# A depthwise sum held in one PSUM bank, strip by strip, and class sums that share one bank

## The reference: what is computed

```python
x = x + _L0_conv_ref(_gn(x), W_v, W_a, b_a, W_o, b_o)   # outlook attention
x = x + _L1_conv_ref(_gn(x), w)                         # depthwise 3 x 3, weights binarized
# inside _L0: v = x @ W_v; a = softmax(pool2x2(x) @ W_a + b_a) over 9 of 9 x 9 x 12 logits
#             out = a @ patches(v), folded back by overlap-add into y; y @ W_o + b_o
# inside _L1: k = sign(clip(w, -1, 1)); out = conv(x, k, 3 x 3, 'SAME', one filter a channel)
# _gn: (v - mean) / sqrt(var + eps) over groups of 3 channels of one image
```

## Time and profile before

| | |
|---|---|
| median of 3 runs | 5118.91 us |
| the profiled execution, its span | 5120.9 us |
| VectorE busy | 4730.3 us, 92% |
| TensorE busy | 4119.3 us, 80% |
| GpSimd busy | 4037.2 us, 79% |
| ScalarE busy | 2005.6 us, 39% |
| TensorE's granted clock, mean | about 0.85 of full speed |

### The profile page before, as it was taken

The page is one execution under the profiler, slowest core; times in us unless marked ns, Lnnn a source line. Parts: engine busy times, 40 slices in busy tenths (PEclk is TensorE's granted clock), DMA queues, the critical chain, the costliest instruction groups (busy, mean ns, idle before and its releaser), DMA issues.

```text
span 5120.9 us, 55367 instructions
## 1 busy us (share of the span) xinstructions
PE 4119.3 (80%) x13632; PEld 2114.1 (41%) x13632; DVE 4730.3 (92%) x3723; ACT 2005.6 (39%) x2753; POOL 4037.2 (79%) x3628
## 2 busy tenths in 40 slices
PE   4877887878887888878788887888878888878885
PEld 2434444434444344444344443444434444434442
DVE  5799999999999999999999999999999999999997
ACT  4424444334443344432444433444324444334431
POOL 5787877877877888778878788787787787887883
PEclk7988888888888788888888888888888888888887
DMA  1110111101111111111011111111110111111111
GB/s 39 38 38 24 47 44 37 47 21 40 47 33 47 36 25 47 42 39 47 21 40 47 33 47 30 31 47 38 43 47 15 46 47 33 47 24 37 47 29 28
DMA packets 126083, 194.36 MB, mean 38 GB/s; under 512 B 14248, under 2 KB 115464, under 8 KB 122472
## 3 DMA queue, kind: packets, MB, share of 16 engines
q1 hardware_dynamic: 97384, 155.50, 13.0%
q10 hardware_dynamic: 28672, 38.55, 2.5%
HBM read 39.22 MB, written 38.54 MB: 15 GB/s over the span
## 4 chain that ended last, share of the span: by engine, by line
POOL 45%; issue 25%; PE 18%; ACT 5%; DVE 5%; DMA 1%; SPq 0%; DVEq 0%; POOLq 0%; ACTq 0%; PEldq 0%; PEld 0%
POOL prod L363 15%; POOL part L356 10%; POOL att L351 10%; PE acc L753 10%; POOL att L345 6%; PE bc L733 4%; DVE prod L600 2%; ACT X L440 2%; POOL pc L332 2%; PE side L698 2%; ACT X L523 2%; PE side L692 1%; DVE ACC L647 1%; PE side L710 1%; DVE top L631 1%
## 5 line engine op out<-in xcount | busy, mean ns | idle before, releaser
L753 PE MATMUL acc<-prod,wo 96*96 96x392 f32 x5312 | 2478.5, 573 | 161.8 <-POOL prod L363 155.7
L600 DVE TENSOR_TENSOR prod<-bc,VAL 96x784 f32<-96x784 f32 x2048 | 1928.2, 959 | 307.5 <-PE bc L733 289.4
L363 POOL TENSOR_TENSOR prod<-prod 96x392 f32<-96x392 f32 x1440 | 1685.5, 1178 | 501.3 <-DVE prod L600 491.7
L733 PE MATMUL bc<-stack,sel 96*96 96x392 f16 x4608 | 1303.2, 378 | 633.5 <-DVE prod L600 611.5
L647 DVE SCALAR_TENSOR_TENSOR ACC<-XP,sg,ACC 96x1064 f32<-96x1064 f32 (+1 forms) x768 | 1736.2, 2281 | 14.9 <-ACT ACC L534 13.8
L753 PEld LDWEIGHTS acc<-prod,wo 96*96 96x96 f32 x5312 | 982.1, 188 | 675.1 <-issue 271.6
L733 PEld LDWEIGHTS bc<-stack,sel 96*96 96x96 f16 x4608 | 576.2, 137 | 1571.4 <-DVE prod L600 972.2
L351 POOL TENSOR_TENSOR att<-att,top 108x420 f32<-108x420 f32 (+1 forms) x576 | 750.3, 1321 | 38.3 <-ACT top L467 38.3
L345 POOL TENSOR_TENSOR att<-att,top 108x420 f32<-108x420 f32 (+1 forms) x576 | 645.1, 1138 | 144.2 <-DVE top L623 144.2
L356 POOL TENSOR_TENSOR part<-att,part 108x420 f16<-108x420 f32 (+1 forms) x576 | 737.3, 1298 | 0.0
L433 ACT ACTIVATE att<-side,ba 108x420 f32<-108x420 f32 (+1 forms) x576 | 340.5, 597 | 671.6 <-PE side L698 659.0
(11 more groups left out here) (55 smaller groups left out, 2183.7 us busy)
## 6 DMA issues: line engine op xcount, KB each, us to landing
stack<-part SPq DMA_DIRECT2D x192, 275.3 KB
stack<-part SPq DMA_DIRECT2D x192, 256.9 KB
tok_in<-in_x SPq DMA_DIRECT2D x32, 1176.0 KB, 9.7
out<-tok_out ACTq DMA_DIRECT2D x224, 168.0 KB, 4.2
stack<-part SPq DMA_DIRECT2D x192, 30.5 KB
stack<-part SPq DMA_DIRECT2D x192, 28.5 KB
X<-in_L_conv_W_a SPq DMA_DIRECT2D x1, 364.5 KB
ACC<-select SPq DMA_DIRECT2D x1, 144.0 KB
```

The lines of the kernel that those rows point to most:

```text
L363: nc.gpsimd.tensor_tensor(p[:, 0, :], p[:, 0, :], p[:, 1, :], ALU.add).then_inc(pre_added, 1)
L600: nc.vector.tensor_tensor(prod[:, g % PRODUCTS, :, :].rearrange("c a (i j) -> c a i j", j=WIN), b, v, ALU.mult).then_inc(prod_ready, 1)
L733: last = nc.tensor.matmul(bc[g % 2][0:CH, a, 0:UNIT], sel[:, which, :], stack[h][:, qi, ki * TAPS + kj, si:si + HALF, sj:sj + WIN], start= ...
L753: last = nc.tensor.matmul(acc[c % 2][0:CH, 0:UNIT], wo[:, :], prod[:, g % PRODUCTS, a, :], start=first, stop=s == LAST[c] and (g in PRE or ...
```

## The change: what it does

- A PSUM bank `strip` takes the place of one of the two `acc` banks. The image's 56 rows become seven strips of eight rows. For each strip ScalarE writes the centre tap from ACC into `strip`, seven taps read XP (SBUF) and `strip` (PSUM) and write `strip`, and the eighth writes ACC (SBUF). That is 56 tap instructions of 448 elements a partition in place of 24 of 1064 or 1008, and 7 centre taps in place of 3.
- All strips use the same bank. So each tap waits for the tap just before it, and the centre tap of a strip waits for the last tap of the strip before.
- The centre taps stand in slots 12, 18, 24, ..., 48; the taps of a strip in the five slots behind, two in every second one (13, 13, 14, 15, 15, 16, 17, 17, and so on to 53).
- All classes share the one bank `acc`. TensorE begins class c only when class c-1 has been added to X1. Classes 0 and 2 end inside a slot whose second half already belongs to the next class; a new semaphore `class_ended` tells VectorE of that moment, and `add_class` comes one slot earlier (slots 15, 22, 30 of a half in place of 16, 23, 31).

```diff
--- before.py
+++ after.py
@@ -36,6 +36,7 @@
          for c, (pr, pc) in enumerate(CLASSES) for rv, rows in AXIS[pr] for cv, cols in AXIS[pc]]
 SLOTS = len(TERMS) // 2
 LAST = [max(n for n, t in enumerate(TERMS) if t[0] == c) // 2 for c in range(4)]
+MID = [c for c in range(3) if TERMS[2 * LAST[c] + 1][0] != c]
 BODY = 2 * SLOTS
 LAG = 3
 PRODUCTS = 4
@@ -82,13 +83,14 @@
     "start x1": 4,
     "start acc": 1,
     "rimmed": 10,
-    "centred": (12, 14, 15),
-    "taps": (14, 17, 18, 18, 19, 20, 20, 21, 25, 29, 30, 31, 32, 34, 35, 45, 48, 48, 48, 50, 50, 52, 53, 53),
+    "centred": (12, 18, 24, 30, 36, 42, 48),
+    "taps": (13, 13, 14, 15, 15, 16, 17, 17, 19, 19, 20, 21, 21, 22, 23, 23, 25, 25, 26, 27, 27, 28, 29, 29, 31, 31, 32, 33, 33, 34, 35, 35, 37, 37, 38, 39, 39, 40, 41, 41, 43, 43, 44, 45, 45, 46, 47, 47, 49, 49, 50, 51, 51, 52, 53, 53),
 }
 PRE = [g for g in range(BODY)
        if TERMS[2 * (g % SLOTS)][0] == TERMS[2 * (g % SLOTS) + 1][0] and g not in AT["not pre"]]
-CUTS = (0, 19, 38, SIDE)
-TAP_N = 3 * (KK - 1)
+STRIP = 8
+STRIPS = SIDE // STRIP
+TAP_N = STRIPS * (KK - 1)
 assert len(AT["taps"]) == TAP_N
 
 
@@ -175,7 +177,8 @@
         shift = sb("shift", [CH, 2])
 
         bc = [ctx.enter_context(nc.psum_tensor(f"bc{b}", [128, 2, 512], F32)) for b in range(2)]
-        acc = [ctx.enter_context(nc.psum_tensor(f"acc{b}", [128, 512], F32)) for b in range(2)]
+        acc = ctx.enter_context(nc.psum_tensor("acc", [128, 512], F32))
+        strip = ctx.enter_context(nc.psum_tensor("strip", [128, 512], F32))
         side = [ctx.enter_context(nc.psum_tensor(f"side{b}", [128, 512], F32)) for b in range(2)]
 
         weights_in = sem("weights_in")
@@ -185,6 +188,7 @@
         bcast_full = sem("bcast_full")
         prod_ready = sem("prod_ready")
         summed = sem("summed")
+        class_ended = sem("class_ended")
         y_added = sem("y_added")
         side_full = sem("side_full")
         side_read = sem("side_read")
@@ -218,6 +222,8 @@
 
         wa_in = X1[:, :, :].rearrange("c h w -> c (h w)")[:, 0:KK * QN]
         sel_in = ACCf[0:STACKED, 0:SELS * CH].rearrange("r (s c) -> r s c", c=CH)
+
+        stripv = strip[0:CH, 0:STRIP * SIDE].rearrange("c (r w) -> c r w", w=SIDE)
 
         def a4(h):
             return att[h][:, :, :].rearrange("r k (i j) -> r k i j", j=WIN)
@@ -530,8 +536,9 @@
             def centre_tap(i, part):
                 until(act, gn_scale, upto(10, i, 6))
                 until(act, xp_ready, upto(1, i, 1))
-                a = ACC[:, CUTS[part]:CUTS[part + 1], :]
-                nc.scalar.activation(a, a, ACT.Identity, bias=centre[:, 2:3], scale=centre[:, 1:2]).then_inc(centred, 1)
+                until(act, tapped, upto(TAP_N, i, (KK - 1) * part))
+                nc.scalar.activation(stripv, ACC[:, STRIP * part:STRIP * (part + 1), :], ACT.Identity,
+                                     bias=centre[:, 2:3], scale=centre[:, 1:2]).then_inc(centred, 1)
 
             def body(i, s1, s2, cv):
                 more = [(at, smooth, (i - late, *what), smooth_step, s2 if late else s1) for at, late, *what in SMOOTH]
@@ -602,13 +609,16 @@
 
             def add_class(i, h, c):
 
-                until(dve, summed, upto(BODY, i, h * SLOTS + LAST[c] + 1))
+                if c in MID:
+                    until(dve, class_ended, upto(2 * len(MID), i, h * len(MID) + MID.index(c) + 1))
+                else:
+                    until(dve, summed, upto(BODY, i, h * SLOTS + LAST[c] + 1))
                 if h == 0 and c == 0:
                     until(dve, x1_init, upto(1, i, 1))
                 pr, pq = CLASSES[c]
                 r0 = 2 * HALF * h + pr
                 xv = X1[:, r0:r0 + 2 * HALF - 1:2, pq:pq + 2 * WIN - 1:2]
-                nc.vector.tensor_tensor(xv, acc[c % 2][0:CH, 0:UNIT].rearrange("c (i j) -> c i j", j=WIN), xv,
+                nc.vector.tensor_tensor(xv, acc[0:CH, 0:UNIT].rearrange("c (i j) -> c i j", j=WIN), xv,
                                         ALU.add).then_inc(y_added, 1)
 
             def soft(home, what, h, n):
@@ -632,23 +642,24 @@
                 ins.then_inc(soft_step, 1)
 
             def tap(i, n):
-                t, part = divmod(n, 3)
+                part, t = divmod(n, KK - 1)
+                last = t == KK - 2
                 t += t >= KK // 2
                 ty, tx = divmod(t, TAPS)
-                r0, r1 = CUTS[part], CUTS[part + 1]
+                r0, r1 = STRIP * part, STRIP * (part + 1)
                 if n == 0:
                     until(dve, xp_ready, upto(1, i, 1))
 
-                if n < 3:
-                    until(dve, centred, upto(3, i, n + 1))
-                else:
-                    until(dve, tapped, upto(TAP_N, i, n - 2))
-                a = ACC[:, r0:r1, :]
-                nc.vector.scalar_tensor_tensor(a, XP[:, r0 + ty:r1 + ty, tx:tx + SIDE], sg[:, t:t + 1], a,
+                if n % (KK - 1) == 0:
+                    until(dve, centred, upto(STRIPS, i, part + 1))
+                else:
+                    until(dve, tapped, upto(TAP_N, i, n))
+                nc.vector.scalar_tensor_tensor(ACC[:, r0:r1, :] if last else stripv,
+                                               XP[:, r0 + ty:r1 + ty, tx:tx + SIDE], sg[:, t:t + 1], stripv,
                                                ALU.mult, ALU.add).then_inc(tapped, 1)
 
 
-            add_at = {min(LAST[c] + LAG + 1, SLOTS - 1): c for c in range(3)}
+            add_at = {LAST[c] + LAG: c for c in range(3)}
 
             def body(i, s1, s2, cv):
                 plan = [(at, soft, (i - late, *what), soft_step, s2 if late else s1) for at, late, *what in SOFT]
@@ -749,10 +760,12 @@
                     first = t == 0 or TERMS[t - 1][0] != c
                     if first:
 
-                        until(pe, y_added, upto(8, i, 4 * h + c - 1))
-                    last = nc.tensor.matmul(acc[c % 2][0:CH, 0:UNIT], wo[:, :], prod[:, g % PRODUCTS, a, :],
+                        until(pe, y_added, upto(8, i, 4 * h + c))
+                    last = nc.tensor.matmul(acc[0:CH, 0:UNIT], wo[:, :], prod[:, g % PRODUCTS, a, :],
                                             start=first, stop=s == LAST[c] and (
                                                 g in PRE or t == 2 * s + 1 or TERMS[t + 1][0] != c))
+                    if a == 0 and c in MID and s == LAST[c]:
+                        last.then_inc(class_ended, 1)
                 last.then_inc(summed, 1)
 
             def body(i, s1, s2, cv):
@@ -765,6 +778,7 @@
                     elif s1 and s == 0:
                         skip(pe, bcast_full, SLOTS)
                         skip(pe, summed, SLOTS)
+                        skip(pe, class_ended, len(MID))
                     if g < LAG and cv:
                         add_up(i - 1, BODY + g - LAG)
                     for n, use in enumerate(USES):
```

## The result

The changed kernel takes 5268.72 us (median of 4 runs, 5259.82 to 5275.11) against 5117.11 for the kernel before in the same comparison (4 runs, 5112.86 to 5120.16): 1.0298 times as long, 95% interval 1.0284 to 1.0313. It is slower, where 4850 us and faster were forecast. The profiled execution's span is 5266.6 us.

The account below looks back on a forecast made before the run. VectorE was taken to bound the tap stretch, TensorE partly the rest. 26.0 - 3.8 - 2.4 - 5.7 - 3.2 - 2.0 = 8.9 us saved a pass, 276 in 31 passes, plus 12 in the last: 4857, stated as 4850; range 4780 to 4930.

Parts of the forecast that it names:

- Collision goes: VectorE's taps with two SBUF sources and GpSimd stop holding each other up: gain 24.5 us a pass.
- taps: 56 taps of 448 elements at 0.67 us, 0.60 start to start, replace 24 longer ones: cost 3.8 us a pass.
- order within a strip: 21 taps a pass stand directly behind the tap they need, 0.12 us each: cost 2.4 us a pass.
- a tap through PSUM is slow: Rival: reading and writing the same bank costs two cycles an element, tap 1.13 us, about 5660 us; chance 0.06.
- the collision stays: Rival: collision lies in the read of XP alone, so 26 us a pass do not return, 5650 us; chance 0.02.
- Centre taps and the single strip: VectorE waits for ScalarE's centre taps in slots 31, 36, 43 and 49: cost 5.7 us a pass, bounds 2 and 9.
- TensorE in slots 20 to 23: TensorE needs 10.1 us there, VectorE's new work is 7.6: a new wait of 2.0 us a pass.
- One bank for the classes: TensorE waits for class additions, then VectorE idles, in slots 30, 62 and 54: cost 3.2 us a pass, bounds 1 and 6.
- The last pass: Taps alone, without GpSimd work, go from 30.9 to 43.2 us: cost 12 us.
- TensorE takes over: Rival: TensorE's clock falls after each new wait and holds broadcasts, another 5 us a pass, about 5000 us; chance 0.17.
- The waits are covered: Rival: waits and TensorE's shortage cost half, dependent pairs nothing, 16.7 us a pass saved, 4610 to 4750 us; chance 0.24.

Follow-up runs that it names:

- run 8: Changed kernel's strips and tap order, but each strip summed in SBUF and classes in two PSUM banks: 5615.83 us, 1.0972 of the kernel before.
- run 1: Kernel before with only the single class bank and additions of classes 0 to 2 one slot earlier, taps in SBUF: 5467.93 us, 1.0675.
- run 2: Changed kernel without class waits, three of four additions a half replaced by an unused reduction (output not the reference's): 4936.83 us, 0.9639 of the kernel before.
- run 9: Changed kernel plus 17 unused matmuls a pass ahead of the slots at the lower clock: 5203.87 us, 1.0135 of the kernel before.
- run 7: Changed kernel with class end ahead of the broadcast, four centre taps moved, and logit and value blocks moved: 4877.39 us, 0.9543 of the kernel before.
- run 4: Changed kernel with four of seven centre taps moved to slots 26, 37, 41 and 47: 5081.07 us, 0.9918 of the kernel before.

## Why the prediction was wrong

- *Collision goes, taps, order within a strip*: right. Forecast -24.5 + 3.8 + 2.4 = -18.3 us of VectorE's work a pass, measured -18.1. A tap is 677 ns (forecast 0.67). The rival "a tap through PSUM is slow" falls, and "the collision stays" too (run 8 shows what brings it back).
- The Trainium skill's larger fixed cost for PSUM ("VectorE: DVE Perf Modes", errata section) does not show: 0.68 us of 448 elements at 0.96 GHz leave 0.21 fixed for PSUM, and with SBUF alone, in run 8, the taps that meet no collision take the same (the median is 681 ns). The 0.12 us of a dependent pair is borne out as well. Slot 13, one product and two taps of one strip, is 2.20 us long: 0.88 + 0.60 + 0.60 + 0.12. By the Trainium skill's semaphore that costs nothing ("The DRAIN you can't avoid") it would be 2.08.
- *Centre taps and the single strip* (5.7, measured 5.2) and *TensorE in slots 20 to 23* (2.0, measured 2.0): right. Three of the four centre taps come out within 0.03 us, slot 49 at 1.18 instead of 1.6. The text of the second counts seven taps; six stand in these slots, and its 7.6 us is the sum with six.
- *One bank for the classes* is the step that failed. It said 3.2 us a pass, with 1 to 6 as bounds. It is 11.0 alone (run 1) and 10.2 within the change (run 2), both above the upper bound; slots 30, 47, 62, 55 and 3 by themselves hold 9.1. That is some 7 us a pass too little, or 210 in 30 passes. The slot of the main wait and its chain were right. The size was taken from matmuls at full clock, and in slots 30, 47 and 62 TensorE is at the lower level. It fell there in slots 28, 45 and 58, ahead of the class waits. The clock explains 3.1 us in slots 47 and 62 (run 9). And slot 47 was taken as covered by its two taps, which it is not (1.75), and slot 3, 0.86 more than before, was not priced.
- *Slot 48* has no term: 3.6 us a pass, some 105 in all. Those logits were hidden behind the three taps that stood in slot 48, the 10.85 us of the earlier trace rows. Free of collisions these three would still be 3.7 us long, an estimate from the 1.24 us of a free tap, so the cover went with their place as well as with the collision. Run 8, with collisions, two class banks and no tap in slot 48, idles 0.80 there, and run 7, with the logits moved, 0.74. The prediction asked what each new wait costs, not which old work of TensorE loses its cover when the taps shrink and move.
- *The end of a pass* has no term either: slot 63 idles 2.26 us instead of 0.47. VectorE's next instruction comes late behind the branch, and the trace shows instruction loads in each pass that the kernel before does not have. All runs with 56 taps have these loads and 2.1 to 3.7 us of idle time in slot 63; run 1 has no such loads and 1.40. That the longer program is the cause is the likely reading; no run tests it alone.
- Together 7.0 + 3.6 + 1.8 = 12.4, against the 12.2 us by which the idle time went past its forecast (21.6 against 9.4: 5.7, 3.2 and 2.0, less the 1.5 swallowed). That it comes out so close is in part luck: run 2 also takes 0.6 us out of slot 48, which is counted twice, and the centre taps cost 0.5 less than forecast.
- *The last pass*: forecast +12, the taps +14.9. The first passes and the last with products, +27 together, had no term.
- The rival "TensorE takes over" (0.17) came nearest. It had the falling clock, but as a result of the new waits and for 5 us a pass. The clock falls ahead of them, the runs show 3.1 us for it in two slots, and the miss is more than twice the rival's price. "The waits are covered" is refuted by run 4, where removing 4.4 us of waits for centre taps made the pass 6.1 shorter.

Open: why slot 30 would not take the full clock in run 9, how a pass would go with every slot at full clock, and what the late instruction at the end of a pass costs when nothing else changes.

## What to carry to other kernels

When a change shortens the engine that bounds, list for each slot what the other engines did under the time that goes or moves; that work is the next bound and no wait in the code names it. A buffer given up is paid in a chain of two engines in turn, priced with TensorE at the clock of that very place, which was 0.50 here at a mean of 0.83. Look at the turn of the loop too, when an engine's program grows. Here the same strips give 4.8% when the class end goes first, the centre taps stand where ScalarE is free, and the logits are spread.

## What was unexpected of the hardware

TensorE's granted clock stands at or near 0.50 in the same slots of each pass (29 and 30, 45 to 47, 59 to 62). It falls where TensorE has waited 4.46, 2.63 and 1.24 us for VectorE or ScalarE, a slot or more ahead of the class ends that then pay for it. A few matmuls whose results nobody reads made the changed kernel 65 us faster in run 9. VectorE's sequencer stands 2.7 us at the end of each pass of the longer program, and 0.25 in the shorter one. And the same strips left in SBUF (run 8) were worse than the large parts before: the taps' busy time is 1972 us against 1736, with single taps of 448 elements at up to 6.37 us, beside seven instructions of GpSimd.
